# Attention loop: score tiles in two groups around another pair's value product, output product ahead of the value projection, GpSimd's sums without a wait

## What is computed

```
mod = (_silu(L0_c) @ L0_wmod).reshape(L0_c.shape[0], 6, 1, -1)
...
h = _layernorm(x, axis=-1) * (1 + ca) + sa
x = x + ga * _L0_attn_ref(h, L0_attn_W_qkv, L0_attn_W_out)
h = _layernorm(x, axis=-1) * (1 + cb) + sb
x = x + gb * _L0_ffn_ref(h, L0_ffn_gate_w, L0_ffn_expert_bias, L0_ffn_w_up, L0_ffn_w_down)
```

```
q = rotary_embedding(q, seq_len, HEAD_DIM)
k = rotary_embedding(k, seq_len, HEAD_DIM)
...
scores = jnp.einsum('bqhd,bkhd->bhqk', q, k) * scale
...
scores = jnp.where(mask, scores, NEG_INF)
weights = jax.nn.softmax(scores, axis=-1)
out = jnp.einsum('bhqk,bkhd->bqhd', weights, v)
```

## Time and profile before

| what | us |
|---|---|
| median of 3 runs | 996.21 |
| lowest and highest | 993.32, 998.24 |
| profiled execution, its own time | 990.0 |
| its span | 988.2 |
| PE busy in the span | 903.2 |
| DVE busy | 770.1 |
| ACT busy | 743.5 |
| POOL busy | 570.8 |

### The profile page before, as it was taken

One profiled execution on the slowest core, in us unless ns is written; L12 is line 12 of the kernel. 1 busy time (PEld: TensorE's weight loads), 2 busy tenths in 40 slices (PEclk: granted clock), 3 DMA queues, 4 the chain that ended last, 5 costly groups with the idle time before them and its releaser, 6 DMA issues. The chain is left out here.

```text
span 988.2 us, 21752 instructions
## 1 busy us (share of the span) xinstructions
PE 903.2 (91%) x6278; PEld 657.7 (67%) x6278; DVE 770.1 (78%) x2328; ACT 743.5 (75%) x2070; POOL 570.8 (58%) x687
## 2 busy tenths in 40 slices
PE   4699999999999999999999999999999878999920
PEld 3467667676776677777767677677676556888820
DVE  7577777777877787877778778777887679899847
ACT  4488878878787887788778878787878755777725
POOL 1445456645666467657765764657566356765532
PEclk9999999999999999999999999999999989999975
DMA  8234443334344434433343344343333357999844
GB/s 258 84 94 105 111 110 98 95 94 105 95 111 117 116 97 119 118 97 95 109 114 96 102 122 119 101 114 112 106 94 96 98 199 269 311 317 331 296 143 128
DMA packets 124580, 135.78 MB, mean 137 GB/s; under 512 B 13837, under 2 KB 108443, under 8 KB 120496
## 3 DMA queue, kind: packets, MB, share of 16 engines
q1 hardware_dynamic: 118768, 122.61, 42.8%
q0 software_dynamic: 4544, 8.93, 2.7%
q10 hardware_dynamic: 1152, 2.85, 0.8%
HBM read 51.72 MB, written 39.49 MB: 92 GB/s over the span
## 5 line engine op out<-in xcount | busy, mean ns | idle before, releaser
L1357 POOL TENSOR_TENSOR four<-four 128x512 f32<-128x512 f32 x128 | 161.2, 1280 | 276.1 <-DMA four<-four 138.8
L1276 DVE CUSTOM_DVE_ANT_0 ps<-ps,tri 128x512 f32<-128x512 f32 (+3 forms) x512 | 239.0, 520 | 73.2 <-PE ps L1070 73.1
L1172 ACT ACTIVATE prob<-ps,nmax 128x512 f32<-128x512 f32 (+3 forms) x512 | 264.7, 534 | 4.1 <-DVE nmax L1276 3.3
L1091 PE MATMUL ps<-ident,prob 128*128 128x128 f32 x1280 | 191.1, 279 | 6.5 <-ACT prob L1172 2.4
L1091 PEld LDWEIGHTS ps<-ident,prob 128*128 128x128 f32 x1280 | 142.8, 141 | 55.5 <-ACT prob L1172 26.4
L1361 POOL TENSOR_TENSOR qk_lo<-four,qk_hi 128x512 fp32r<-128x512 f32 x128 | 163.1, 1296 | 0.1
L1193 ACT COPY probt<-ps 128x512 f32<-128x512 f32 (+2 forms) x256 | 125.2, 522 | 41.1 <-PE ps L1091 41.1
L1113 PE MATMUL ps<-probt,val 128*64 128x512 f32 (+3 forms) x1024 | 152.0, 439 | 0.2 <-ACT probt L1193 0.2
L1200 ACT CAST qk_hi<-four 128x512 fp32r<-128x512 f32 x128 | 79.4, 620 | 94.3 <-POOL four L1357 92.8
L1263 DVE TENSOR_TENSOR four<-ps,turn_s 128x1024 f32<-128x1024 f32 x64 | 78.4, 1225 | 54.8 <-PE ps L1035 50.3
L1113 PEld LDWEIGHTS ps<-probt,val 128*64 128x64 f32 x1024 | 67.8, 136 | 73.7 <-issue 59.5
(11 more groups left out here) (276 smaller groups left out, 2234.9 us busy)
## 6 DMA issues: line engine op xcount, KB each, us to landing
four<-four SPq DMA_DIRECT2D x252, 128.0 KB
wt<-parts SPq DMA_DIRECT2D x24, 1024.0 KB, 6.7
slots<-fill SPq DMA_DIRECT2D x64, 288.0 KB, 2.8
parts<-split SPq DMA_DIRECT2D x64, 128.0 KB, 2.3
wq_lo<-parts SPq DMA_DIRECT2D x6, 1024.0 KB, 6.3
hb<-h_hi SPq DMA_DIRECT2D x64, 64.0 KB, 2.3
hb<-h_lo SPq DMA_DIRECT2D x64, 64.0 KB, 2.0
plain<-results SPq DMA_DIRECT2D x8, 512.0 KB, 7.5
```

The source lines that it names most:

```text
L1091: mm = e.transpose(ps[:, PT + at % 2, at_block * P:(at_block + 1) * P], prob[:, unit, kk * P:(kk + 1) * P], ident[:])
L1172: e.activation(prob[:, unit, 0:w], ps[:, bank_s(idx) + j, 0:w], ACT.Exp, bias=nmax[:, q.par, idx, j:j + 1], scale=-1.0, accum_out=den[:, q ...
L1276: e.tensor_tensor_reduce(block_, block_, tri[:, S - w:S], -1.0, HIGHEST, ALU.add, ALU.min, nmax[:, q.par, idx, j:j + 1]).then_inc(v_max, 1)
L1357: e.tensor_tensor(qk[:, cols], tt[:, cols], ur[:, cols], op=ALU.add).then_inc(g_qk, 1)
```

## The change

PE's order becomes: projection of k, turn 0, projection of q, turns 2a, 2b and 1, sums, score tiles 0 and 1, values, score tiles 2 and 3, turns 3a and 3b, output product, value projection, `route_pe`. The sums go to bank 6 instead of W1. ScalarE computes all eight exponentials of q1 in one slot and copies turns 0, 2a, 2b and 1; VectorE copies 3a and 3b, behind the residual sum. The wait ahead of `route_pe` therefore is for VectorE's copy of 3a. GpSimd no longer waits for `dve_ot` ahead of its sums.

```
             def pe_turn_prob(e, q, u):
                 n, at = q.n, TURNS.index(u)
                 e.wait_ge(a_exp, NU * n + READ[u][-1] + 1)
                 if u == "3a":
-                    if due(2 * n):
-                        e.wait_ge(v_ev, 2 * n)
+                    if due(4 * n - 1):
+                        e.wait_ge(a_ev, 4 * n - 1)
+                    if due(n):
+                        e.wait_ge(a_r, n)
                 elif u == "3b":
                     if due(4 * n):
                         e.wait_ge(a_ev, 4 * n)
-                elif u == "2a":
-                    e.wait_ge(v_ev, 2 * n + 1)
+                elif u in ("0", "2a"):
+                    e.wait_ge(v_ev, 2 * n + {"0": 1, "2a": 2}[u])
                 else:
-                    e.wait_ge(a_ev, 4 * n + {"0": 1, "2b": 2, "1": 3}[u])
+                    e.wait_ge(a_ev, 4 * n + {"2b": 1, "1": 2}[u])
...
             def pe_turn_sum(e, q):
                 e.wait_ge(a_rep, q.n + 1)
-                e.wait_ge(v_tk, min(q.n + 3, STEPS))
+                e.wait_ge(a_ev, 4 * q.n + 3)
                 for i in range(TB):
-                    mm = e.transpose(ps[:, W1, i * P:(i + 1) * P],
+                    mm = e.transpose(ps[:, PT, i * P:(i + 1) * P],
...
                 if q0.live:
-                    pe_qk(e, q0)
+                    pe_k(e, q0)
                 if q2.live:
                     spare_read(e, i, c - 1)
                     pe_turn_prob(e, q2, "0")
+                if q0.live:
+                    pe_q(e, q0)
+                if q2.live:
                     pe_turn_prob(e, q2, "2a")
-                if q1.live:
-                    pe_scores(e, q1, 0)
-                if q2.live:
                     pe_turn_prob(e, q2, "2b")
                     pe_turn_prob(e, q2, "1")
                     pe_turn_sum(e, q2)
                 if q1.live:
+                    pe_scores(e, q1, 0)
                     pe_scores(e, q1, 1)
                 if q2.live:
                     pe_values(e, q2)
                 if q1.live:
+                    pe_scores(e, q1, 2)
+                    pe_scores(e, q1, 3)
                     pe_turn_prob(e, q1, "3a")
-                    pe_scores(e, q1, 2)
+                    pe_turn_prob(e, q1, "3b")
                 if q2.live:
                     pe_out(e, q2)
-                if q1.live:
-                    pe_turn_prob(e, q1, "3b")
                 if v.live:
                     pe_v(e, v)
                 if c in SPARE:
                     if q1.live:
-                        e.wait_ge(a_ev, 4 * q1.n + 1)
+                        e.wait_ge(v_ev, 2 * q1.n + 1)
                     elif q2.live:
-                        e.wait_ge(v_ev, 2 * q2.n + 2)
+                        e.wait_ge(a_r, q2.n + 1)
                     route_pe(e, i, c)
-                if q1.live:
-                    pe_scores(e, q1, 3)
...
                 if q2.live:
-                    act_exp(e, q2, 5)
-                    act_exp(e, q2, 6)
-                    act_exp(e, q2, 7)
                     act_store(e, q2, "0")
+                    act_rep(e, q2)
                     act_store(e, q2, "2a")
-                    act_rep(e, q2)
+                    act_store(e, q2, "2b")
                     act_store(e, q2, "1")
                     act_r(e, q2)
...
                 if q2.live:
                     dve_acc(e, q2)
                 if q1.live:
+                    dve_store(e, q1, "3a")
                     dve_store(e, q1, "3b")
...
                 if q0.live:
-                    if q2.live and i and c:
-
-                        e.wait_ge(v_ot, q2.n + 1)
                     pool_qk(e, q0, 1)
                     pool_qk(e, q0, 0)
```

More of the change, by code:

```diff
@@ L1030, in pe_qk, with pe_q @@
                 e.matmul(ps[:, W1, :], wq_hi[:, k_cols], h_lo[:, cols_of(q.b)], start=False, stop=True)
+            def pe_q(e, q):
+                n = q.n
                 e.wait_ge(a_v, min(n + 2, NV))
@@ L1209, in act_r @@
                     e.wait_ge(v_ot, q.n)
-                e.copy(rs[:], ps[:, W1, :]).then_inc(a_r, 1)
+                e.copy(rs[:], ps[:, PT, :]).then_inc(a_r, 1)
             def act_rep(e, q):
@@ L1244, in act_slot @@
                     act_v(e, v)
+                if q1.live:
+                    for unit in range(4, NU):
+                        act_exp(e, q1, unit)
                 if q0.live:
                     act_hi(e, q0, 1)
-                    act_hi(e, q0, 0)
                 if v.live and (i, c) != (0, 2):
                     act_v(e, v)
+                if q0.live:
+                    act_hi(e, q0, 0)
                 if (i, c) == (0, 1):
                     group_root(e, 1, s_var, s_root)
-                if q1.live:
-                    act_exp(e, q1, 4)
                 route_act(e, i, c)
@@ L1287, in dve_store @@
                 e.wait_ge(p_t, 6 * n + TURNS.index(u) + 1)
-                if u == "3b" and due(n - 1):
+                if u == "3a" and due(n - 1):
                     e.wait_ge(p_vp, n - 1)
@@ L1323, in dve_slot @@
                     n_factors(e)
-                if q2.live:
-                    dve_store(e, q2, "2b")
                 if q1.live:
-                    dve_peak(e, q1, 0)
-                    dve_peak(e, q1, 1)
-                    dve_peak(e, q1, 2)
-                    dve_peak(e, q1, 3)
+                    for unit in range(4):
+                        dve_peak(e, q1, unit)
                 route_dve(e, i, c)
@@ L1336, in dve_slot @@
                 if q1.live:
-                    dve_peak(e, q1, 4)
-                    dve_peak(e, q1, 5)
+                    for unit in range(4, NU):
+                        dve_peak(e, q1, unit)
                 if q2.live:
```

44 lines of the change are left out of this document (18 added, 26 removed).

## The result

The changed kernel takes 1011.6 us (median of 4 runs, 1010.0 to 1012.7), the kernel before 995.9 (median of 4, 993.3 to 998.2). The ratio is 1.0157, with a 95% interval from 1.0128 to 1.0186: 1.6% slower. The forecast was 1017, 2.1% slower, with a range from 995 to 1036.

The account below looks back on a forecast made before the run. PE was taken to bound the loop; -0.63 + 0.40 + 0.55 = +0.32 us a slot, times 64 slots +20.5 us, gave 1017 us against the median 996.2, 2.1% slower, with a range from 995 to 1036.

Parts of the forecast that it names:

- What bounds the kernel: PE bounds the loop, busy 595.84 of 600 us; 11.69 us a slot, 11.27 without router work.
- Term A: PE's reordered score tiles: fewer openings and closings of tile runs save 0.63 us a slot.
- prediction's sign of being wrong: Forecast is wrong if PE idles under 20 us, merged tiles save much more than 0.4 us, or another group waits longer.
- rule of the Trainium skill: Changing tiling mode drains TensorE; nine changes a slot become four, also giving -0.63 us.
- Term B: New PE wait ahead of turn 1 for ScalarE's copy of turn 2a: +0.40 us a slot.
- Term C: Slot's end: PE waits 0.77 us for VectorE's copy of 3a in five slots, 0.17 for the residual sum in three.
- The sum: -0.63 + 0.40 + 0.55 = +0.32 us a slot, times 64 slots +20.5 us.
- rival 3: Slower still: costlier hand-overs to PE, and turn 0 waits for ScalarE's reading of router's rows; +24 us, 1041 us; chance 0.12.
- The parts at nothing: GpSimd's earlier sums and the shifted ScalarE and VectorE work were booked at no change in time.
- ScalarE's slack: ScalarE, 486 of 600 us busy, was taken to have room for all eight exponentials in one slot.
- Rival 1: Faster: the slot's end does not wait, -0.23 us a slot, -15 us, 981 us; chance 0.15.
- The clock: PE's idling lowers the granted clock; a tenth lost over the loop costs some 70 us; chance 0.03.

Follow-up runs that it names:

- e4_tiles_apart: Changed kernel with turn 3a put between score tiles 2 and 3, undoing that one merging; ratio to the kernel before 1.0355, loop 772.2 us.
- e7_before_merged: Kernel before with only score tile 3 moved right behind tile 2, both ahead of turn 3a; ratio 0.9986, loop 737.0 us.
- e9_tile0_between: Changed kernel with score tile 0 between turns 2b and 1, and tile 1 behind the sums; ratio to the kernel before 1.0191, loop 759.2 us.
- e1_copy_3a_early: Changed kernel with VectorE's copy of turn 3a between the peaks of tiles 2 and 3, ahead of the residual sum; ratio to the kernel before 1.0105.
- e3_gpsimd_wait: Changed kernel with GpSimd's wait for the normalisation put back ahead of its sums; ratio to the kernel before 1.0144, loop 752.8 us.

## Why the forecast held, step by step

**What bounds the kernel.** PE's start-to-start times made the slot, and the mean slot times 63 the loop: 11.94 - 11.69 = 0.25, times 63 is 15.8 us, which is the loop's +16.1 and the medians' +15.7.

**Term A** was -0.63 us; it measured 10.48 - 11.27 = -0.79. The mechanism is shown by e4_tiles_apart, where undoing one of two mergings costs 0.31, and by e7_before_merged, where moving tile 3 up to tile 2 shortens the undisturbed slot by 0.43. The 0.43 is larger because there turn 3a also loses the score tile behind it and the value projection too, as the prediction's own pieces say: 0.20 + 0.11 + 0.10 = 0.41. The two runs of tiles take 1.18 and 1.07 us in the slot above, where I had 1.21 and 1.08. The prediction's sign of being wrong, merged tiles that save much more than 0.4, did not show: 0.89 + 0.48 - 1.18 = 0.19 and 0.73 + 0.55 - 1.07 = 0.21. Most of the missing 0.16 lies in the turns and the output product: turns 3a and 3b and the product take 0.93 + 0.81 = 1.74, where I had 1.82, and turn 0 between the projections takes 0.14 of PE, not 0.23. The size was off, not the step. The rule of the Trainium skill ("TensorEngine Tiling (Array Packing)", Key Properties), counted as nine changes of mode to four, gave the same -0.63; the experiments agree with it in sign. At 0.31 for the two changes that e4_tiles_apart adds, 0.155 each, five would give 0.78, near the 0.79; and e7_before_merged, which by the same count takes three away, gives 0.14 each.

**Term B** was +0.40 and measured 0.45, in 54 of 54 slots. In e9_tile0_between, with tile 0 as cover, no turn waits for ScalarE's copy any more.

**Term C** was +0.77 and +0.17 us and measured 0.85 and 0.25, the mean 0.62 for 0.55 (the term's heading says 0.56; the sum uses 0.55). The chain came out as written, a sum 1.09 (not 1.20) behind the start of the product, but the next group starts 0.81 us behind the product, not 0.99, so PE stood there earlier. That the wait for the copy is VectorE's order is shown by e1_copy_3a_early, where it goes. The smaller wait for the residual sum was read from the trace alone; no run takes it away.

**The sum.** -0.79 + 0.45 + 0.62 = +0.28 a slot, and the router and the small waits are 0.39 (11.94 - 10.48 - 0.45 - 0.62) instead of 0.42: +0.25. Errors of -0.16, +0.05, +0.07 and -0.03 left 0.07 below the forecast of +0.32. Part of this is luck: the saving of term A was put too small and so were the two waits, and the errors took each other off. So is the 0.39 for 0.42, which I had booked as the same in both kernels. The small waits of before are gone (the loads of the turns for exponentials, 19.9 us, those of q for the value copy, 7.2), and others came: from start to start, turn 0 now waits for ScalarE's work on the router's bank for 0.34, 0.24 and 0.23 us in slots 0, 3 and 5 on the mean. That is rival 3's mechanism at about its booked size, 0.3 us in two slots of eight. Against the median I added 20.5 and measured 15.7.

**The parts at nothing.** GpSimd's wait: shown by e3_gpsimd_wait. ScalarE's slack is the step that does not hold as I put it. I took ScalarE's idle share of the window as its slack. Between 60 and 700 us the idle time lies mostly ahead of the exponentials, behind VectorE's peaks (80.4 us), and ahead of the copies of turns, behind PE (49.2); at the slot's end its queue is full, and the router's read, the rounding of q and the value copy are all on the edge. The changed kernel paid little for it, because PE was late itself. Rival 1 rested on the same mistake: with the copy of 3a early, the kernel is not 15 us below the kernel before, but its loop is 13 us longer (749.4 against 736.4).

**The clock.** The granted clock stayed at 1.00 from 100 to 700 us with PE 93% busy. It did fall at the loop's two ends, to 0.88 from 27 to 100 us and 0.86 from 770 to 830 us (1.00 and 0.94 before), that is, for part of these stretches PE ran at 1.2 in place of 2.4 GHz. What sets that off in these stretches stays open: e1_copy_3a_early, with the same order of PE, has 1.00 in the first of the two, and e3_gpsimd_wait 0.88. From the first k projection to the eighth the changed kernel takes 81.7 us and e1_copy_3a_early 81.5, but their waits differ in this stretch, so I can't separate what the clock costs there, nor its share in the drain's 5 us.

**Left open.** Whether a version clearly faster than before exists. e7_before_merged is at 0.9986 (0.9961 to 1.0011), no measurable gain; its short slots show 0.43 us a slot to be won, if ScalarE's end of the slot can be emptied first.

## What to carry to other kernels

Cost a new order of the bounding engine in both coins: what its instructions save from start to start, and for each wait that it moves, how much of the engine's own work is left between the release and the wait. Here a saving of 0.8 us a slot in the matmuls' order was real and was more than paid away, by 0.45 us because a copy lost its cover and by 0.62 because a sum moved ahead of a copy. And a wait that is removed uncovers the next one: look at what the other engines have in their queues at that point of the slot, not at their idle share.

## What the runs showed that I had not expected

A run of score tiles that use half of the array's rows costs less than its parts, and the saving follows the number of changes between such matmuls and others: 0.31 us for two changes (e4_tiles_apart), 0.43 for three (e7_before_merged). And PE's busy time in the profile fell by 28 us with the same instructions while the kernel got slower. The busy time of PE holds time in which overlapping matmuls wait (of the 0.45 us ahead of turn 1 the row shows 0.33 as idle), so it says little about how much work there is.
